# Row maxima in feed-forward's stretch taken as whole quads of four matmuls instead of threes

## The reference

```python
q, k = rope(xn @ Wq.T), rope(xn @ Wk.T)          # 16 sub-heads of 8
probs = softmax(q @ k.T)                         # 1024 x 1024 for each sub-head
diff = probs[:, 0::2] - lam * probs[:, 1::2]     # 8 heads
attn = rms_norm(diff @ v) * (1 - LAMBDA_INIT) @ Wo.T
w = top-3 of 8 zones for each batch, from tanh(mean(xn) @ W1 + b1) @ W2 + b2
ffn = xn + sum over zones e of w[e] * (gelu(xn @ Wa[e]) @ Wb[e])    # 512 wide inside
```

## Time and profile before

| | us |
|---|---|
| median of 3 runs | 475.67 (475.26 to 476.3) |
| the profiled execution's own time | 473.91 |
| its span | 472.1 |
| PE busy in the span | 432.7 |
| DVE busy | 385.4 |
| ACT busy | 332.2 |
| POOL busy | 131.9 |
| mean granted TensorE clock | 0.967 |

### The profile page before, as it was taken

The page is one execution under the profiler, slowest core; times in us unless marked ns, Lnnn a source line. Parts: engine busy times, 40 slices in busy tenths (PEclk is TensorE's granted clock), DMA queues, the critical chain, the costliest instruction groups (busy, mean ns, idle before and its releaser), DMA issues.

```text
span 472.1 us, 7272 instructions
## 1 busy us (share of the span) xinstructions
PE 432.7 (92%) x2623; PEld 192.8 (41%) x2623; DVE 385.4 (82%) x726; ACT 332.2 (70%) x430; POOL 131.9 (28%) x154
## 2 busy tenths in 40 slices
PE   7396599999999899999999999999999999999987
PEld 6385355666666423323333333333333333322235
DVE  2788278999898969998999999999999998986225
ACT  1431255555555478889888988898889888989972
POOL 4157699978686400000001001000001000000000
PEclk9597799999999979999999999999999999999999
DMA  8507863200000040002000201000000000000002
GB/s 308 205 1 237 314 258 120 95 28 20 3 1 1 6 175 1 2 2 91 3 1 1 91 25 67 3 1 1 2 3 1 3 1 1 1 2 3 1 0 90
DMA packets 12038, 25.65 MB, mean 54 GB/s; under 512 B 1250, under 2 KB 5986, under 8 KB 11874
## 3 DMA queue, kind: packets, MB, share of 16 engines
q1 hardware_dynamic: 11570, 22.37, 13.6%
q10 hardware_dynamic: 432, 2.81, 1.6%
HBM read 15.48 MB, written 9.44 MB: 53 GB/s over the span
## 4 chain that ended last, share of the span: by engine, by line
PE 60%; ACT 10%; issue 9%; DVE 8%; POOL 5%; DMA 4%; SPq 2%; ACTq 0%; POOLq 0%
PE ps L1019 19%; PE ps L989 16%; PE ps L1012 10%; ACT E L573 8%; DVE part_max L734 6%; PE ps L952 3%; DMA X<-in_x 3%; POOL hL L440 2%; PE ps L870 2%; PE ps L953 2%; PE ps L954 2%; PE ps L872 2%; PE ps L871 2%; POOL rope L406 1%; DMA q_scr<-ropeL 1%
## 5 line engine op out<-in xcount | busy, mean ns | idle before, releaser
L734 DVE TENSOR_REDUCE part_max<-ps 128x1 f32<-128x512 f32 x512 | 319.5, 681 | 37.0 <-PE ps L989 33.6
L573 ACT ACTIVATE E<-ps 128x1024 f32<-128x1024 f32 x256 | 245.9, 1027 | 38.0 <-PE ps L1012 37.2
L1019 PE MATMUL ps<-E,Vg 128*32 128x512 f32 x1024 | 138.1, 612 | 1.2 <-ACT E L573 1.1
L989 PE MATMUL ps<-K,Q 32*128 32x512 f32 x384 | 110.8, 477 | 3.3 <-DVE part_max L734 2.8
L1012 PE MATMUL ps<-Q,K 32*128 32x512 f32 x384 | 88.9, 485 | 7.0 <-ACT E L573 5.3
L989 PEld LDWEIGHTS ps<-K,Q 32*128 32x128 f32 x384 | 46.6, 184 | 93.3 <-DVE part_max L734 89.4
L440 POOL TENSOR_TENSOR hL<-h,hH 128x512 fp32r<-128x512 f32 x48 | 61.4, 1288 | 12.3 <-ACT hH L545 11.6
L543 ACT ACTIVATE h<-ps 128x512 f32<-128x512 f32 x48 | 28.6, 597 | 38.2 <-PE ps L872 24.9
L1012 PEld LDWEIGHTS ps<-Q,K 32*128 32x128 f32 x384 | 36.2, 184 | 37.3 <-ACT E L573 33.2
L478 POOL TENSOR_TENSOR U<-AT,rsum 128x256 f32<-128x256 f32 x15 | 9.3, 621 | 145.1 <-DVE rsum L789 136.3
L431 POOL CAST neg_max<-neg_f 128x16 fp32r<-128x16 f32 x16 | 3.1, 197 | 118.0 <-DVE neg_f L743 118.0
(11 more groups left out here) (148 smaller groups left out, 418.3 us busy)
## 6 DMA issues: line engine op xcount, KB each, us to landing
k_scr<-ropeH SPq DMA_DIRECT2D x6, 512.0 KB, 5.0
K<-k_scr SPq DMA_DIRECT2D x6, 512.0 KB, 4.5
Q<-q_scr SPq DMA_DIRECT2D x6, 512.0 KB, 5.8
tab<-in_tables ACTq DMA_DIRECT2D x1, 2048.0 KB, 11.2
q_scr<-ropeL SPq DMA_DIRECT2D x4, 512.0 KB, 5.6
q_scr<-ropeH SPq DMA_DIRECT2D x4, 512.0 KB, 6.7
wa_raw<-in_wa SPq DMA_DIRECT2D x6, 256.0 KB, 2.8
wb_raw<-in_wb SPq DMA_DIRECT2D x6, 256.0 KB, 3.2
```

The lines of the kernel that those rows point to most:

```text
L573: nc.scalar.activation(E[:, par, 2 * jj:2 * jj + 2, :].rearrange("p j t -> p (j t)"), ps[:, 2 * jj:2 * jj + 2, :].rearrange("p j t -> p (j ...
L734: nc.vector.tensor_reduce(part_max[:, tile // FC % 2, j * FC + tile % FC, sh:sh + 1], ps[:, SLOT_BANK[quad_slot(t) + k], :], AX.X, ALU.max ...
L989: mm(ps[:, SLOT_BANK[x], :], Qs[g % KQ_BUFS][strip(j), tile % TB * P:(tile % TB + 1) * P], Ks[g % KQ_BUFS][strip(j), sh * BANK:(sh + 1) * ...
L1019: last = mm(ps[QUAD * j:QUAD * (j + 1), B_PV, :], Vg[:, par, st, j // 2, :], E[:, s % 2, k, :], start=(st == 0), stop=(st == TB - 1), skip ...
```

## The change

The same 36 lead quads are kept whole. `lead_block(t)` gives quad t the half step 8t/3, rounded down, of 96: half step 2n is `first(n + 3)`, 2n + 1 is `second(n)`. The four matmuls of a quad stand together behind that half step, behind `first` where it is even and behind `second` where it is odd. So three quads go to four units, with 2, 3 and 3 half steps between them, where each unit had three slots. The order of the reads on VectorE follows, as do the places of `half_negate` on GpSimd, and the ring's bank table (which changes from quad 16 on).

```diff
--- before.py
+++ after.py
@@ -61,8 +61,7 @@
 
 KQ_OWN, KQ_BUFS = 3, 5
 
-LEAD_BANKS = 3
-LEAD = UNITS * LEAD_BANKS // GJ
+LEAD = 36
 SLOTS = 2 * ALL_UNITS + 2 * GROUPS
 
 MAX_STEPS = 116
@@ -89,16 +88,21 @@
     return min(33 * hx + 44, SLOTS - 1)
 
 
-def lead_slots(n):
-
-    return [divmod(x, GJ) for x in range(n * LEAD_BANKS, (n + 1) * LEAD_BANKS)]
-
-
-def lead_ring(t, k):
+def lead_block(t):
+
+    return 2 * UNITS * t // LEAD
+
+
+def lead_quads(block):
+
+    return [t for t in range(LEAD) if lead_block(t) == block]
+
+
+def lead_ring(t):
 
     if t >= LEAD:
         return RING
-    n = (GJ * t + k) // LEAD_BANKS
+    n = lead_block(t) // 2
     return (4, 5, 2, 3) if n < 22 else (4, 5, 3, 0) if n < 26 else (4, 5, 0, 1)
 
 
@@ -108,7 +112,7 @@
     for t in range(QUADS):
         extra = (t % 8 == 2 and t > 2) + (t == QUADS - 1)
         for k in range(GJ + extra):
-            bank = min(lead_ring(t, min(k, GJ - 1)), key=lambda b: last.get(b, -1))
+            bank = min(lead_ring(t), key=lambda b: last.get(b, -1))
             before.append(last.get(bank))
             last[bank] = len(banks)
             banks.append(bank)
@@ -121,8 +125,8 @@
 
 def last_lead_slot(banks, steps=UNITS):
 
-    t, k = lead_slots(steps - 1)[-1]
-    return max(x for x in range(quad_slot(t) + k + 1) if SLOT_BANK[x] in banks)
+    quads = sum(lead_block(t) < 2 * steps for t in range(LEAD))
+    return max(x for x in range(quad_slot(quads)) if SLOT_BANK[x] in banks)
 
 
 def max_slots(s):
@@ -455,8 +459,8 @@
                     wa_zone(e)
                 if n % UZ == 5 and e < PICKS:
                     wb_zone_low(e)
-                for t, k in lead_slots(n - 3) if n >= 3 else ():
-                    if t % TB == TB - 1 and k == GJ - 1:
+                for t in lead_quads(2 * n - 5) + lead_quads(2 * n - 6):
+                    if t % TB == TB - 1:
                         half_negate(t // TB)
 
 
@@ -771,8 +775,9 @@
                                                ALU.mult, ALU.add).then_inc(comb_done, 1)
 
             for n in range(UNITS):
-                for t, k in lead_slots(n):
-                    reduce_slot(t, k)
+                for t in lead_quads(2 * n) + lead_quads(2 * n + 1):
+                    for k in range(GJ):
+                        reduce_slot(t, k)
                 if n % UZ == 2 and n // UZ + 1 < PICKS:
                     wb_zone(n // UZ + 1)
 
@@ -1033,12 +1038,16 @@
                     first(a)
                 if n == 0:
                     pe.wait_ge(rot_done, 4 * BATCH * CB)
-                for t, k in lead_slots(n):
-                    max_slot(t, k)
+                for t in lead_quads(2 * n):
+                    for k in range(GJ):
+                        max_slot(t, k)
                 if n % UZ == 0:
                     pe.wait_ge(wb_split, n // UZ + 1)
                 pe.wait_ge(hl_done, n + 1)
                 second(n)
+                for t in lead_quads(2 * n + 1):
+                    for k in range(GJ):
+                        max_slot(t, k)
             pe.wait_ge(qmax_in, 32)
             pe.wait_ge(slot_read, last_lead_slot((0, 1)) + 1)
             pe.sem_inc(e_free, 2)
```

## The result

The changed kernel takes 478.75 us (median of 6, 477.52 to 479.17) against 475.07 for the kernel before (median of 6, 473.45 to 476.3). The ratio is 1.0088 with a 95% interval of 1.007 to 1.0106: 3.7 to 4.2 us slower. The prediction was 4.7 slower, 480.4, with a range of 471.5 to 484.5.

What follows compares the result with a forecast made beforehand. TensorE was taken to bound feed-forward by 0.13 us a unit. Plain cycles of 75.1 and extras of 4.5 put unit 44 5.1 later; the tail returned 0.4: 475.67 + 4.7 = 480.4 us, range 471.5 to 484.5.

Steps and rivals of the forecast that it cites:

- The cycle: Feed-forward from unit 9 to 44: three quads per four units repeat every 8.58 us, against 8.08 before.
- the loop of waits: TensorE and VectorE wait in turn over three quads: 2.71 + 0.53 + 2.51 + 0.12 + 2.71 = 8.58 us.
- The holds: TensorE's waits for a quad's last bank in each cycle, 0.45 us at one quad and 0.69 at the next.
- The extras: Feed-forward time above the plain cycles, from start_sum, half_transpose and wb_zone: 4.5 us against 3.8 before.
- wb_zone: Four on VectorE behind a quad's reads, each moving reads by 0.4 us, with late gelu 0.05 more: sum 1.8.
- start_sum and the transposes: Feed-forward: two start_sum pairs cost 0.9 us and three half_transpose 1.8 us.
- The rival of a falling clock: TensorE's standing lowers the clock in feed-forward; one stretch costs at most 3.4 us, giving 483.8; chance 0.07.
- the prediction's signs of being wrong: Quads pass in 0.64 us without standing, four matmuls not side by side, or granted clock under 1 in 80 to 165.
- The GpSimd-bound start: Before 80.64 us GpSimd sets the pace, so quads 0 to 6 cost nothing; uncovered they would cost 1.0 us.
- The tail: From unit 44's group to attention's start: 7.7 us against 8.09, giving 0.4 back.
- the half-clock stretch: Lower clock behind feed-forward, taken to repeat; if it goes, up to 3.4 us come back.
- The faster rival: Engines don't wait in turn if a quad's last bank is free when TensorE comes: 470.4, 469 to 473; chance 0.18.

Runs made afterwards that it cites:

- wb_zone early: Changed kernel with wb_zone on VectorE one unit earlier: 476.0 us, ratio 1.0023; the kernel before with the same move: 474.02 us, 0.9989.
- short reads: In lead quads VectorE reads only 256 of 512 columns of each maximum: the kernel before takes 470.15 us, the changed kernel 465.3 us.
- five banks: Sums of both chunks share one bank, giving the ring a fifth during most of feed-forward: kernel before 472.34 us, changed kernel 474.89 us.
- whole quads behind first layers and wb_zone late: Changed kernel with odd-half-step quads moved to the next even one, wb_zone behind the same quads as in the changed kernel: 484.64 us, ratio 1.0223.
- five banks and wb_zone early: Fifth ring bank plus wb_zone on VectorE one unit earlier: changed kernel 471.69 us, ratio 0.9958; kernel before with both edits 472.57 us, 0.9966.

## Why the prediction was right

- **The cycle.** Forecast 8.58 us for four units, measured 8.51; the loop of waits is as written. The 0.07 is the read spacing. It is 0.60 from one read to the next, and it was so in the kernel before; the 0.627 was a misreading, since the 6.90 us of eleven reads hold the last one's full 0.68 and a step of 0.82 at 155.74, where VectorE waited for the next group. Over 8.75 cycles that makes 74.5 us plain, where the prediction had 75.1. The holds were forecast as 0.45 and 0.69, the profile has 0.33 and 0.70.
- **The extras** (what the stage takes above its plain cycles) were the term that was mis-sized. Forecast 4.5 us, measured 79.80 - 74.5 = 5.3. The term in it that was too small is wb_zone: 1.8 were given for four zones, and its move alone gives back 3.1 in the same stretch. For start_sum and the transposes 2.7 were given, and with wb_zone early all extras together are 76.71 - 74.5 = 2.2; they were not measured one by one. The prediction said that TensorE's stand would hide ScalarE's late hH but for 0.05 us a zone; in the profile `first` waited 4.4 us in seven places.
- **The clock.** The rival of a falling clock came in part, after the 1.47 us stand shown above, and with it one of the prediction's signs of being wrong: the granted clock from 80 to 165 us was 0.98, not 1.00. Windows of the changed kernel:

```profile
91.00:97.00 6.00, 5.13 (x21) 3.44 (x21) 3.26 (x6) 2.71 (x6) 3.95 (x4) 0.72 0.20 77
97.00:165.00 68.00, 64.28 (x281) 40.10 (x281) 58.86 (x101) 36.94 (x69) 50.24 (x47) 1.00 0.03 9
```

  Granted 0.72 over 91 to 97, which is 3.4 us at 1.2 GHz: matmuls at 93.82 and 94.25 last 0.63 and are 0.43 apart. From unit 16's maxima-bearing `first` to unit 18's it took 6.32 us; with wb_zone early, where the clock held, 4.90. So this spell cost at most 1.4 us of the 3.1, 1.2 of it in six steps from matmul to matmul (93.25 to 95.95, 2.70 us where 0.33 + 5 x 0.23 = 1.48 is usual), against an upper bound of 3.4 put on such a stretch. Without it the extras would have been some 3.9, under the forecast. The stands of 0.33 and 0.70 us in each cycle left the clock at 1.00 for the 68 us after 97. Whether the one long stand brought the clock down is not shown: a stand of 1.45 us in another kernel did not (see the last section).
- **The GpSimd-bound start** hid the first seven quads as said: 24.70 against 24.66 us.
- **The tail** gave 0.2 back, not 0.4. Attention was untouched, and the half-clock stretch at its start came again as assumed (0.77 granted from 165 to 180 us, 6.9 us at the lower level; 6.8 before).
- **Sum.** From unit 0 to the first score +5.0 us, against +4.7 forecast. The medians moved by 3.7, since the profiled execution of the changed kernel was its longest of six (479.17) and that of the kernel before (473.91) was shorter than its median. That the two errors (a shorter cycle, larger extras) have opposite signs is luck. The 480.4 also rested on a median of three for the kernel before, 475.67; that of six is 475.07.
- **The faster rival** fell, but its condition was the right one: with short reads a quad's last bank is free when TensorE comes, and there whole quads win by 4.85 us, 3.8 of them in the stage.

## What to carry to other kernels

Before grouping work to save switches between kinds of matmul, write down the ring of buffers: if one group takes all its buffers, the producer's last step must wait for the consumer's last one, and then uneven gaps make the two wait in turn though each has slack on average. Follow one period by hand with start times, the answer delay and the hand-over; that gave 8.58 where 8.51 was measured. And look what else queues on the consumer: a small instruction placed behind a full train of reads is late for everyone who waits for it, and moving it by one unit was worth more than half of the loss. Last, compare by stage and by ratio: with short reads and with five banks, 1 us of the difference in the totals lay behind the first score, in a stretch of lower clock that one of the two kernels didn't have in full.

## What the runs showed of the hardware

- In the changed kernel wb_f, from on-chip memory to on-chip memory, took 1.25 us at 87.95 while GpSimd's hL ran from 87.64 to 88.92, and 0.47 at 144.43 with GpSimd idle. Reads of PSUM were not slowed beside hL: the four from 151.27, with hL at 151.41, took the usual 2.48. The Trainium skill's "SBUF — State Buffer", SBUF: two separate sides, says that a pair of ports shared by GpSimd and VectorE (for a VectorE instruction in one of its 2-port modes, or with two inputs from on-chip memory) is locked for a whole instruction by whichever starts first, and that the other is fully blocked. That the long wb_f ended only after hL agrees with it. It ended 0.28 us after, less than the 0.47 it takes by itself, so not all of it stood behind hL; no row shows in which mode it ran.
- Four matmuls on four 32-row strips took TensorE no more than three (0.51 against 0.50, and 0.44 to the next full matmul against 0.43).
- A stand of TensorE is no sure sign of a lower clock. In the changed kernel one of 1.47 us was followed by 3.4 us at the lower level between 91 and 97 us, while those of up to 0.7 us in each cycle and one of 1.05 at 71.50 were not. With the fifth bank a stand of 1.05 us (71.30 to 72.35) was followed at once by such a spell (0.62 granted from 72.0 to 76.5). And these two, the first with whole quads behind first layers and wb_zone late, the second with five banks and wb_zone early, left the clock at 1.00 from 60 to 90 and from 62 to 90 us:

```profile
73.78 0.48 PE L875 MATMUL ps<-xnH,waH 128*128 128x512 f32 x1 [1.45 <-ACT hH L549]
```

```profile
80.32 0.47 PE L959 MATMUL ps<-hH,wbH 128*128 128x512 f32 x1 [1.51 <-POOL hL L444]
```
